# A fused attention and feed-forward kernel on eight cores: smaller SBUF arenas, six plus two PSUM banks, and the feed-forward blocks in pairs of token chunks

## What is computed

```python
xn = _layernorm(x, axis=-1)
q  = xn @ Wq + bq                       # 16 heads of 64
kv = (xn @ Wdown + bdown) @ Wup + bup   # latent 256, then k and v
att = softmax(q k^T / 8)                # 16 x 16 per token, over heads
attn = (att v) @ Wout + bout
gate = silu(act_quant(xn) @ ternary(w_gate)^T)
up   = act_quant(xn) @ ternary(w_up)^T
ffn  = act_quant(gate * up) @ ternary(w_down)^T
out  = x + attn + ffn
```

## Time and profile before

| | us |
|---|---|
| median of the two runs shown | 7627.73 (7576.08 and 7679.39) |
| profiled execution, device time | 7536.99 |
| its span, slowest core | 7535.4 |
| spans of the other cores | 7469.1 to 7508.3 |
| mean granted TensorE clock, by core | 0.763 to 0.773 |
| PE busy | 4203.5 (56%) |
| DVE busy | 1623.7 (22%) |
| ACT busy | 943.4 (13%) |

### The profile page before, as it was taken

The page is one execution under the profiler, slowest core; times in us unless marked ns, Lnnn a source line. Parts: engine busy times, 40 slices in busy tenths (PEclk is TensorE's granted clock), DMA queues, the critical chain, the costliest instruction groups (busy, mean ns, idle before and its releaser), DMA issues.

```text
span 7535.4 us, 48227 instructions; the slowest of 8 cores (7469.1 to 7535.4 us)
## 1 busy us (share of the span) xinstructions
PE 4203.5 (56%) x14462; PEld 2018.4 (27%) x14598; DVE 1623.7 (22%) x2954; ACT 943.4 (13%) x1032; POOL 294.4 (4%) x388
## 2 busy tenths in 40 slices
PE   0110267736774477735773577646773677447764
PEld 0000124312332234312431233212431233123421
DVE  3333313121122202121212211121312112221212
ACT  0110120010201020101101020102001120102010
POOL 0000001000000001000100001000100000000100
PEclk9999996758777676767776776867686777767786
DMA  5444401422023202321132202321142213220232
GB/s 150 126 139 139 142 31 34 139 76 84 29 93 110 84 23 75 115 87 58 34 117 89 78 17 84 123 97 32 34 151 73 78 31 102 96 84 23 84 123 90
DMA packets 382203, 635.91 MB, mean 84 GB/s; under 512 B 120193, under 2 KB 252545, under 8 KB 375554
## 3 DMA queue, kind: packets, MB, share of 16 engines
q1 hardware_dynamic: 235906, 506.95, 20.9%
q10 hardware_dynamic: 137856, 109.06, 4.3%
q0 software_dynamic: 8192, 16.79, 0.7%
HBM read 506.91 MB, written 109.05 MB: 82 GB/s over the span
## 4 chain that ended last, share of the span: by engine, by line
issue 23%; PEldq 19%; DVE 19%; DMA 15%; PEld 14%; ACT 5%; DVEq 2%; ACTq 1%; POOLq 1%; POOL 0%; SPq 0%
PEldq L157 18%; PEld pd L766 4%; DMA arena<-gpscr 3%; DMA arena<-arena 3%; DVE arena L795 3%; PEld pd L465 2%; DMA arena<-tdT 2%; DVE qsc L820 2%; ACT arena L841 2%; DVE arena L871 1%; PEld pd L896 1%; PEld pd L655 1%; DVE arena L617 1%; DVE dnst L609 1%; DVE arena L848 1%
## 5 line engine op out<-in xcount | busy, mean ns | idle before, releaser
L766 PE MATMUL pd<-arena,kqT 128*128 128x512 bf16 x4008 | 1039.4, 424 | 325.4 <-DVEq L157 314.7
L766 PEld LDWEIGHTS pd<-arena,kqT 128*128 128x128 bf16 x4096 | 433.1, 107 | 938.3 <-issue 622.8
L863 PE MATMUL pd<-identb,arena 128*128 128x128 bf16 x1024 | 149.9, 301 | 932.6 <-DVEq L157 932.6
L702 PE MATMUL pd<-wring,arena 128*128 128x512 f32 x1024 | 544.6, 681 | 169.4 <-DMA arena<-arena 156.7
L896 PE MATMUL pd<-arena 128*128 128x512 bf16 x2000 | 478.7, 390 | 88.8 <-DMA arena<-tdT 69.3
L465 PE MATMUL pd<-arena,wring 128*128 128x512 f32 x1024 | 473.7, 617 | 23.1 <-issue 13.1
L795 DVE SCALAR_TENSOR_TENSOR arena<-pd,qsc,arena 128x512 f32<-128x512 f32 x256 | 192.2, 751 | 1187.8 <-ACTq L157 1155.6
L603 POOL TENSOR_TENSOR arena<-arena,emask_s 128x512 f32<-128x512 f32 x128 | 162.0, 1266 | 6261.3 <-ACTq L157 3116.3
L289 PE MATMUL pd<-identb,arena 128*128 128x128 bf16 x768 | 112.4, 301 | 490.9 <-DVEq L157 490.9
L863 PEld LDWEIGHTS pd<-identb,arena 128*128 128x128 bf16 x1024 | 89.2, 126 | 995.2 <-issue 995.2
L702 PEld LDWEIGHTS pd<-wring,arena 128*128 128x128 f32 x1024 | 210.6, 216 | 494.4 <-issue 494.4
(11 more groups left out here) (81 smaller groups left out, 3306.1 us busy)
## 6 DMA issues: line engine op xcount, KB each, us to landing
wring<-wo SPq DMA_DIRECT2D x128, 512.0 KB, 3.9
arena<-tgT SPq DMA_DIRECT2D x64, 1024.0 KB, 5.5
arena<-tuT SPq DMA_DIRECT2D x64, 1024.0 KB, 8.0
gpscr<-arena ACTq DMA_DIRECT2D x64, 1024.0 KB, 6.0
arena<-gpscr SPq DMA_DIRECT2D x32, 2048.0 KB, 7.9
arena<-tdT SPq DMA_DIRECT2D x128, 512.0 KB, 3.7
arena<-wg SPq DMA_DIRECT2D x64, 512.0 KB, 3.9
arena<-wup SPq DMA_DIRECT2D x64, 512.0 KB, 3.8
```

The lines of the kernel that those rows point to most:

```text
L702: T.matmul(PD[tc][:, 512 * hf:512 * (hf + 1)], ach[:, 128 * tc:128 * (tc + 1)], wring[cp % 2][:, 512 * hf:512 * (hf + 1)], start=(cp == 0) ...
L766: T.matmul(PD[2 * mat + t // 2][:, 512 * (t % 2):512 * (t % 2) + 512], kqT.rearrange("p (i t) -> p i t", t=TILE)[:, i, 128 * t:128 * (t + 1)],
L863: T.transpose(bank[:, 128 * b:128 * (b + 1)], k2[:, 128 * blk:128 * (blk + 1)], identb[:, :])
```

## The change

No arithmetic is changed. Buffers and the order are:

- **SBUF.** `wd_s` and `wu_s` are no longer kept: in every tile `Wdown` is loaded in 2 pieces and `Wup` in 4, of 512 KB each, into `wring`, which now has 4 buffers. The mask product is done in place, so `m1s` is gone. The bf16 buffers (`kq2T`, gate-up blocks, `k2`, `tdring`) move into an arena of their own; the gate-up blocks overlap no attention buffer any more, so their first loads no longer wait for the partition shifts (SH0, SH1).
- **PSUM.** Six fp32 banks and two bf16 banks (`PDB`) in place of eight. Transposes of bf16 data use `PDB`, 8 blocks a round in the prep stage. The flip reuses the bank of q k^T, so q k^T of step s waits for the flip of step s-2 to be copied out.
- **Q** runs in two waves of 4 banks. Wq is loaded twice, and wave 1 waits for ACT's copies of wave 0.
- **Gate-up** does 2 chunks at a time (`tp`): 32 matmuls into 4 banks, 2 silus, 2 products, and PE waits for these before the next 32.
- **Prep and down** go by pairs of chunks: prep of chunks 0 and 1, down for these with all 16 pieces of `tdT`, then the same for 2 and 3. `tdT` is read twice, and a piece serves 8 matmuls. ACT's scaling goes in four pieces of 1024.

```diff
-    wring = [en(nc.sbuf_tensor(f"wring{i}", [128, D], F32)) for i in range(2)]
+    wring = [en(nc.sbuf_tensor(f"wring{i}", [128, D], F32)) for i in range(4)]
...
-    PD = [en(nc.psum_tensor(f"pd{i}", [128, 1024], F32)) for i in range(4)]
+    PD = [en(nc.psum_tensor(f"pd{i}", [128, 1024], F32)) for i in range(3)]
+    PDB = en(nc.psum_tensor("pdb", [128, 2048], BF16))
...
-    for q in range(8):
-        dma("sync", "LDC", wd_s[:, DL * q:DL * (q + 1)], wd_h[128 * q:128 * (q + 1), :])
-    for q2 in range(2):
-        dma("sync", "LDC", wu_s[:, 2048 * q2:2048 * (q2 + 1)], wu_h[128 * q2:128 * (q2 + 1), :])
...
+        for wave in range(2):
+            for q in range(8):
+                slot = q % 4
...
+                if wave == 1 and q == 0:
+                    W("tensor", "S", m_qev)
...
+        for q2 in range(2):
+            for ch2 in range(2):
+                slot = 2 * q2 + ch2
+                W("sync", "TE", wring_last[slot])
+                lv = dma("sync", "LDW%d" % slot, wring[slot][:, :],
+                         wu_h[128 * q2:128 * (q2 + 1), 1024 * ch2:1024 * (ch2 + 1)])
+                W("tensor", "LDW%d" % slot, lv)
         W("tensor", "S", m_lat)
...
                 if s >= 2:
                     W("tensor", "S", exp_m[s - 2])
+                    W("tensor", "V", diag_m[s - 2])
...
-            else:
-                W("sync", "SH0", cnt["SH0"])
-                W("sync", "SH1", cnt["SH1"])
-                W("sync", "V", m_av_all)
...
+            for tp in range(2):
+                if (ob, tp) != (0, 0):
+                    prev = (ob, tp - 1) if tp == 1 else (ob - 1, 1)
+                    W("tensor", "V", gu[(prev[0], "ev%d" % prev[1])])
...
+                            for tl in range(2):
+                                t = 2 * tp + tl
+                                T.matmul(PD[mat][:, 512 * tl:512 * (tl + 1)],
...
+        for pair in range(2):
+            for tl in range(2):
+                t = 2 * pair + tl
+                if t == 0:
+                    W("sync", "OUTG", m_gpw)
+                else:
+                    W("sync", "V", k2done[t - 1])
+                lv = dma("sync", "LDGP", gprd[:, :], gp_h[128 * t:128 * (t + 1), :])
...
+                for hc in range(4):
...
+            for p in range(16):
+                dsem = "LDD0" if p % 2 == 0 else "LDD1"
+                if p >= 2:
+                    W("sync", "TE", dmm[p - 2])
...
+                        for tl in range(2):
+                            for hf in range(2):
+                                T.matmul(PD[tl][:, 512 * hf:512 * (hf + 1)],
```

More of the change, by code:

```diff
@@ L452, in build_nc @@
         m_qsc = mark("vector", "V")
-        wring_last = [marks.get(("wout_last", it - 1, i), 0) for i in range(2)]
-        for q in range(8):
-            wsem = "LDW0" if q % 2 == 0 else "LDW1"
-            W("sync", "TE", wring_last[q % 2])
-            lv = dma("sync", wsem, wring[q % 2][:, :], wq_h[128 * q:128 * (q + 1), :])
-            W("tensor", wsem, lv)
-            if q == 0:
-                W("tensor", "V", m_pha_v)
-            def fqmm(T, q=q):
-                for c in range(8):
-                    T.matmul(BK(c)[:, :], wring[q % 2][:, 128 * c:128 * (c + 1)],
-                             xnT.rearrange("p (i t) -> p i t", t=TILE)[:, q, :],
-                             start=(q == 0), stop=(q == 7))
-            op("tensor", fqmm)
-            wring_last[q % 2] = mark("tensor", "TE")
@@ L499, in build_nc @@
         m_qodd_s = idev[7]
+        for piece in range(2):
+            slot = piece
+            W("sync", "TE", wring_last[slot])
+            lv = dma("sync", "LDW%d" % slot,
+                     wring[slot][:, :].rearrange("p (i c) -> p i c", c=DL),
+                     wd_h.rearrange("(i p) c -> p i c", p=128)[:, 4 * piece:4 * piece + 4, :])
+            W("tensor", "LDW%d" % slot, lv)
         W("tensor", "S", m_qodd_s)
@@ L503, in flmm @@
                 for q in range(8):
[L504 removed]
+                    T.matmul(BK(c)[:, :],
+                             wring[q // 4][:, DL * (q % 4) + 128 * c:DL * (q % 4) + 128 * (c + 1)],
                              xnT.rearrange("p (i t) -> p i t", t=TILE)[:, q, :],
@@ L523, in fkv @@
                 for q2 in range(2):
-                    T.matmul(bank[:, :], wu_s[:, 2048 * q2 + 128 * c:2048 * q2 + 128 * (c + 1)],
+                    T.matmul(bank[:, :],
+                             wring[2 * q2 + c // 8][:, 128 * (c % 8):128 * (c % 8 + 1)],
                              latT[:, TILE * q2:TILE * (q2 + 1)],
@@ L535, in build_nc @@
             marks[("kvev", it, c)] = mark("scalar", "S")
+        for i4 in range(4):
+            wring_last[i4] = cnt["TE"]
         m_kv = marks[("kvev", it, 15)]
```

448 lines of the change are left out of this document (237 added, 211 removed).

## The result

The changed kernel takes 8084.51 us (median, 7981.33 to 8169.15), the kernel before 7554.08 us beside it on the same chip. The ratio is 1.0625, 95% interval 1.0575 to 1.0675: slower, by more than forecast (7900). The profiled execution took 7991.01 us against 7536.99.

The account below looks back on a forecast made before the run. No engine was taken as the bound: stages stand one behind another, leaving the others idle. 5 + 10 + 14 - 1 + 13 = 41 us a tile, 328 in all, less 12, gave 7853, put at 7900; range 7730 to 8120.

Parts of the forecast that it names:

- if the store ends ACT's waits, or if attention has grown: Two signs in the profile after, in gate-up and attention, that would show the prediction wrong; no size given.
- Attention: Attention stage: q k^T's new wait for the flip copy stays hidden behind other PE work, 0 us a tile, at most 11.
- Q: Q stage in two waves: a second cold start and ACT's copies between, +5 us a tile, bounds +2 and +9.
- Latent and kv: Before kv matmuls: PE waits 8.5 us for four Wup loads, then starts cold; +10 us a tile, bounds +6 and +14.
- Gate-up: Gate-up stage: 16 pauses of 3.0 us, half cooling the clock at 1.7 us each; +14 us a tile, bounds 0 and +46.
- the one on the store: Gate-up's store to gpscr: beside a 2 MB load might add about 1 us to each of 7 pauses; counted as nothing.
- rival C: Gate-up: every pause cools, 7 store waits of 1 us, some groups cold; +38 a tile, 8045 or 8090 us; chance 0.20.
- First gate-up loads: Start of gate-up: first loads no longer wait for the partition shifts, -1 us a tile of at most 3.9.
- Prep and down: Prep and down by pairs: down +30.2 at 2.9 us a piece, less prep, load and result savings; +13 us a tile.
- Startup: Start of the kernel: 3 MB fewer to load before DVE's first operation, -12 us once.
- A: Rival: tdT loads arrive at PE's pace and the clock holds in gate-up; -3 us a tile, about 7545 us; chance 0.03.
- B: Rival: gate-up's 3.0 us pauses cost nothing, all else as forecast; 27 us a tile, 7741 or 7785 us; chance 0.22.

Follow-up runs that it names:

- experiment 3: Kernel before plus only three already-met waits a step on PE's queue in attention (q k^T, flip, product with v): 7572.79 us, attention 134.2 us a tile.
- experiment 1: Gate-up split alone in the kernel before: 7692.14 us; that plus a second staging buffer for the store: 7650.68; changed kernel plus that buffer: 7871.24.
- a_td4: Changed kernel with four buffers for tdT in place of two: 7850.14 us, down 97.6 to 71.2 us a tile.

## Why the prediction was right, and by how much it was short

The direction, the places and most of the sizes held, but the sum was short: 41 us a tile were forecast and 58.8 came, or 316 us on the profiled execution and 454. Two of the signs that I had named for being wrong came true, "if the store ends ACT's waits, or if attention has grown"; the two steps behind them failed.

- **Attention, 0 forecast, +3.4.** Wrong. The step reads "Attention: 0 ... What hides it is the product with v and the v transposes on PE". The copy was hidden, as written; but I priced only what is waited for, and the waits themselves, met long before, cost about 0.11 us each ahead of the flip and of the product (experiment 3).
- **Q, +5 forecast, +5.9.** Right: the pause for the copies of a wave was 9.49 us for my 9.4, and its cold start 3.1 for my 2.9. The doubled loads stayed hidden: no wait of PE in Q is ended by a load of Wq.
- **Latent and kv, +10 forecast, +9.5.** Right, with a pause of 8.54 us for my 8.5.
- **Gate-up, +14 forecast, +23.6.** The step that failed is the one on the store, "that is in the upper bound, and I count nothing". It is 15 to 16 us of the 23.6 (experiment 1). I had both numbers in hand, 7.2 us of matmuls to hide behind and about 8 to land, and put the result into rival C at 1 us for each of 7 blocks. That delay was about right: the store took 8.9 us to land and stretched the pauses by 8 us a tile. What I had no size for is the rest: a pause stretched past 3.5 us was followed by a slowed group every time, so the price is about twice the delay. The other part of that term, "I let half of the 16 pauses cool the clock at 1.7: 13.6", was too high: with the store out of the way a third of the pauses of 3.0 us are followed by a slowed group, and the whole split costs 7 in place of 14. The two errors partly cancel. Of the 127 pauses of 3.0 us that were to be seen there are 120 a core, and 66 of them lie between 2.0 and 3.05.
- **First gate-up loads, -1 forecast, -0.6.** Too small to tell.
- **Prep and down, +13 forecast, +16.9.** Down came to +31.6 for my +30.2 (a piece 3.05 us for 2.9), and a_td4 shows that the loads' wait is 26 of it. A scaling piece took 2.29 us for 2.3 and a round of transposes 2.05 for 2.06, as DVE's two rows and PE's two rows from chunk 0 show (answers to the earlier trace rows):

```profile
2485.06 0.75 DVE L895 TENSOR_SCALAR arenab<-arena,mg 128x1024 bf16<-128x1024 f32 x1 [1.59 <-ACTq L162]
2487.35 0.75 DVE L895 TENSOR_SCALAR arenab<-arena,mg 128x1024 bf16<-128x1024 f32 x1 [1.54 <-ACTq L162]
```

```profile
2494.96 1.01 PE L910 MATMUL pdb<-identb,arenab 128*128 128x128 bf16 x8 [1.04 <-DVEq L162]
2497.01 1.01 PE L910 MATMUL pdb<-identb,arenab 128*128 128x128 bf16 x8 [1.04 <-DVEq L162]
```

  The end gave -14.7, not -17.4: the first matmul of down still waits 1.63 us for the last copy, so 3.2 of the 4.8 were to be had, and chunk 2's maximum waits 1.26 us for its load:

```profile
2576.18 32.82 SPq L156 DMA_DIRECT2D arena<-gpscr  x2
...
2585.93 4.42 DVE L865 TENSOR_REDUCE qsc<-arena 128x1 f32<-128x4096 f32 x1 [1.26 <-DMA arena<-gpscr]
```

- **Startup, -12 forecast, -4.** DVE's first operation did come 11.3 us sooner (30.70 before):

```profile
19.39 0.15 DVE L183 TENSOR_SCALAR mg<-ident 128x1 f32<-128x1 f32 x1 [19.39 <-DMA emask_s<-emask]
```

  But on the mean of the cores the first Q matmul comes only 4 us sooner, so some 7 us are lost again in the preparation of the three weights that lies between. There PE's waits for DVE are 4.5 and 3.1 us longer on the slowest core, in the means and in the transposes of the weights; what makes them longer was not tried.

Of the rivals, A (the loads keep up) is out: two in flight do not. B (a pause of 3.0 us costs nothing) is out too: 46% of such pauses are followed by a slowed group, and 32% where the store stretches none. C named the store, which was real, at +23.6 in all where C had +38; its claim that every pause cools was wrong. That the median, 8084.51, stands next to C's 8090 and within my range is in part luck. C's 65 a tile are 8045 on the profiled execution, which took 7991, and I had put 47 us on top for the median where it lies 94 above; attention and down, which C has as the forecast, make up part of what C had too much in gate-up. With the store at its measured 15 and everything else as forecast the sum would have been 56, and that near to 58.8 only because the 7 too much for the split stands against the 3.4 of the attention and the 3.9 of prep and down.

The Trainium skill's page "TensorE: Matmul & The Clock Gate", section "A second HAM failure mode: psum-queue depth-cycling", spoke against this split: it has small idle times between groups of matmuls make the clock swing and the throughput fall. The trace agrees in kind: the stage's granted clock fell from 0.90 to 0.87, and single groups take 7.07 or 8.4 to 8.8 us. It does not agree with my reading of that section, by which all 16 pauses would cost 1.7 us, 27 a tile; with the store's wait removed the whole split costs 7.

What stays open: Q's 5.9 and the 5 us by which down with four buffers is above 66.0 were not taken apart by a run; by the rows the latter are a second cold start and twice as many gaps of 0.23 us between pieces (16 more, 3.7 us). Why one pause of 2.95 us is followed by a slowed group and the next is not, no run shows. What the smaller arenas and the two-bank `PDB` are worth to a kernel that needs the room was not tried either.

## What to carry to other kernels

When a loop is split so that half the work stands between two waits, look at each transfer that used to be hidden behind the whole and compare its landing with the half: here a load of 3.7 us against 1.9 of matmuls, and a store of 6.0 against 7.2, which became 8.9 once it was issued closer behind the loads. The cure for both was more buffers (two more for `tdT` and one for the store, 26 and 16 us a tile), not fewer bytes. And where PE drains its banks in one go, ask whether the loop can be turned so that each bank is drained beside the matmuls of the next: that, with a second staging buffer, removed 41 us a tile, more than anything else tried here.
